# Two-convolution residual steps and an attention block on one core: the second convolution by six products in plain fp32, one image after the other, and the residual added by accumulating transfers

## What is computed

```python
for _ in range(3):
    t = relu(_conv(x, w1) + b1[None, :, None, None])
    x = x + 1/3 * (_conv(t, w2) + b2[None, :, None, None])
x = relu(x)
qkv = einsum('oc,bchw->bhwo', qkv_w, x)          # 8 heads of 8
k = _ln(k, kln_w, kln_b);  v = _ln(v, vln_w, vln_b)
kv = einsum('bhnd,bhne->bhde', k, v) / N
o = einsum('bhnd,bhde->bhne', q, kv)
u = gelu(einsum('oc,bchw->bohw', o1_w, o + x))
return gelu(einsum('oc,bchw->bohw', o2_w, u) + x)
```

## Time and profile before

| | us |
|---|---|
| median of 3 runs (lowest, highest) | 1809.97 (1804.1, 1812.8) |
| span of the profiled execution | 1808.4 |
| its own time by the clock of the runs | not listed apart; the span is 1.6 under the median and inside the runs' range |
| PE busy | 1760.9 (97% of the span) |
| DVE busy | 1268.9 (70%) |
| ACT busy | 916.9 (51%) |
| POOL busy | 1.8 |

### The profile page before, as it was taken

How to read it: one execution, slowest core, us unless ns; L and a number is a source line. 1 busy time by engine, 2 the same in 40 slices (tenths; PEclk the granted TensorE clock), 3 DMA queues, 4 the chain that set the end, 5 groups by cost and what they waited for, 6 DMA issues and landing times.

```text
span 1808.4 us, 30258 instructions
## 1 busy us (share of the span) xinstructions
PE 1760.9 (97%) x10875; PEld 1613.7 (89%) x10875; DVE 1268.9 (70%) x2481; ACT 916.9 (51%) x1533; POOL 1.8 (0%) x16
## 2 busy tenths in 40 slices
PE   7999999999999999999999999999999999999995
PEld 6998989989899898998989989898899989999884
DVE  4674668857687676876668676696666957679585
ACT  3453636446454464545545455454455545455473
POOL 0000000000000000000000000000000000000000
PEclk9999999999999999999999999999999999999997
DMA  3110002020021101111020110201102010000102
GB/s 56 27 22 0 1 1 48 13 36 3 16 33 24 24 3 25 30 19 24 3 41 14 18 25 1 47 7 24 20 1 48 13 24 13 1 1 13 30 7 47
DMA packets 135415, 36.17 MB, mean 20 GB/s; under 512 B 135116, under 2 KB 135116, under 8 KB 135244
## 3 DMA queue, kind: packets, MB, share of 16 engines
q1 hardware_dynamic: 135164, 33.82, 11.2%
q10 hardware_dynamic: 80, 0.15, 0.0%
HBM read 17.17 MB, written 16.78 MB: 19 GB/s over the span
## 4 chain that ended last, share of the span: by engine, by line
PE 87%; DVE 7%; issue 4%; ACT 1%; DVEq 0%; DMA 0%; ACTq 0%
PE bank L900 27%; PE bank L901 26%; PE bank L902 26%; PE bank L996 3%; PE bank L984 2%; PE bank L986 2%; PE bank L985 2%; DVE v_lo L770 1%; DVE combined L737 1%; DVE combined L741 1%; DVE combined L738 1%; DVE x_lo L770 1%; DVE combined L742 0%; DVE kv L793 0%; PE bank L1014 0%
## 5 line engine op out<-in xcount | busy, mean ns | idle before, releaser
L900 PE MATMUL bank<-x_hi,w_hi 128*128 128x448 f32 (+2 forms) x1440 | 517.2, 359 | 13.9 <-issue 7.4
L901 PE MATMUL bank<-x_lo,w_hi 128*128 128x448 f32 (+2 forms) x1440 | 511.4, 355 | 0.0
L902 PE MATMUL bank<-x_hi,w_lo 128*128 128x448 f32 (+2 forms) x1440 | 511.2, 355 | 0.0
L900 PEld LDWEIGHTS bank<-x_hi,w_hi 128*128 128x128 f32 x1440 | 273.2, 190 | 32.2 <-issue 12.6
L901 PEld LDWEIGHTS bank<-x_lo,w_hi 128*128 128x128 f32 x1440 | 273.4, 190 | 15.1
L902 PEld LDWEIGHTS bank<-x_hi,w_lo 128*128 128x128 f32 x1440 | 272.5, 189 | 15.3
L494 ACT ACTIVATE drain<-bank,b_col 128x448 f32<-128x448 f32 (+1 forms) x160 | 98.1, 613 | 254.7 <-PE bank L902 253.9
L500 ACT ACTIVATE drain<-bank 128x512 f32<-128x512 f32 x256 | 154.8, 615 | 107.3 <-PE bank L902 104.6
L719 DVE TENSOR_TENSOR combined<-drain 128x448 f32<-128x448 f32 (+1 forms) x160 | 95.8, 598 | 105.9 <-ACT drain L494 99.5
L770 DVE TENSOR_TENSOR v_lo<-combined,v_hi 128x896 fp32r<-128x896 f32 (+1 forms) x160 | 165.1, 1032 | 0.3
L900 PE MATMUL bank<-t_hi,w_hi 128*128 128x512 f32 x384 | 156.1, 407 | 0.0
(11 more groups left out here) (144 smaller groups left out, 3259.7 us busy)
## 6 DMA issues: line engine op xcount, KB each, us to landing
x_in<-in_x SPq DMA_DIRECT2D x64, 256.0 KB, 4.7
out<-y SPq DMA_DIRECT2D x120, 128.0 KB, 2.6
out<-drain SPq DMA_DIRECT2D x8, 128.0 KB, 2.7
x_res<-in_L_conv_w ACTq DMA_DIRECT2D x1, 144.0 KB, 2.9
x_res<-in_L_conv_w SPq DMA_DIRECT2D x1, 144.0 KB, 5.1
b_col<-in_L_conv_b SPq DMA_DIRECT2D x4, 0.2 KB, 3.0
g<-in_L_conv_o_w SPq DMA_DIRECT2D x3, 16.0 KB
g<-in_L_conv_qkv_w SPq DMA_DIRECT2D x2, 16.0 KB
```

The lines of the kernel that those rows point to most:

```text
L900: mm(ps, lhs[0], rhs[0], start=first, stop=False)
L901: mm(ps, lhs[0], rhs[1], start=False, stop=False)
L902: return mm(ps, lhs[1], rhs[0], start=False, stop=last)
```

## The change

The order of passes is now step 0 image 0, step 0 image 1, step 1 image 0 and so on: a pass is the 5 chunks of the first convolution and then the second convolution in 2 halves of 16 groups, 7 chunks a pass and 42 a pair. All six passes transform: six inputs give four outputs, so a half is 6 products x 2 stacks = 12 matmuls of 256 columns, each a single matmul in plain fp32, in 3 PSUM units of 4. No high and low parts of t exist any more. DVE makes the six planes of t in two sets (`transform_t`: 21 groups behind chunk 2 of a pass, 12 behind chunk 4; 7 instructions each), and the four outputs of each half (`combine_m`, 8 instructions) into `dx`. POOL then issues a transfer that adds `dx` to `x_res` in SBUF (512 KB each, 12 a pair), and ACT and DVE split the new `x_res` (`refresh_hi`, `refresh_lo`, 1024 elements each) 3 and 4 chunks later. ACT also copies the loaded x into `x_res` (`copy_x`). The two conv-input splits, the attention's arithmetic and the loads and stores stay; the `LATE` table has new chunk numbers.

```diff
-SIZES = ((7, 7, 7, 6, 6), (8, 8, 8, 8))
-AHEAD = (1, 2)
+CONV0_SIZES = (7, 7, 7, 6, 6)
+HALVES = 2
+UNITS = [3 if is_conv1(n) else 1 for n in range(NC)]
+PRODUCTS = (1, 2, 3, 4, 0, 5)
+SETS = ((0, 21), (21, SKEWED))
+SET_AFTER = {2: 0, 4: 1}
+REFRESH = (3, 4)
...
-        (NORMALISE, 0, (4, 5, 7, 8, 10, 10, 11, 11)), (OUTER, 0, (6, 7, 9, 10, 11, 12, 12, 13)),
+        (NORMALISE, 0, (5, 6, 7, 7, 8, 10, 10, 11)), (OUTER, 0, (6, 7, 8, 8, 10, 11, 11, 12)),
...
+            with pool.Fori(0, PAIRS) as i:
+                for number in range(NH):
+                    img, h = number // HALVES % 2, number % HALVES
+                    pool.wait_ge(dx_made, i * NH + number + 1)
+                    pool.sem_inc(add_begun, 1)
+                    nc.gpsimd.dma_start(x_res[img][:, HALF_PX * h:HALF_PX * (h + 1)], dx[h][:, :],
+                                        accum_op=ALU.add).then_inc(x_added[h], 16)
...
+            def refresh_hi(i, number):
+
+                img, step, h = number // HALVES % 2, number // HALVES // 2, number % HALVES
+                act.wait_ge(x_added[h], 16 * (i * PASSES + number // HALVES + 1))
...
+            def convolve_conv1(i, n):
+                g0, size = groups_of(n)
...
+                pe.wait_ge(v_made, i * NH + half_number(n) + 1)
+                for part in range(3):
+                    unit = UNIT[n] + part
+                    bank_free(i, unit)
+                    for k in range(2):
+                        q = PRODUCTS[2 * part + k]
+                        ps = conv_ps[unit % CONV_BANKS][:, k * PLANE:(k + 1) * PLANE]
+                        for stack in range(2):
+                            last = mm(ps, fw[:, q, 1 - stack, :], v_all[:, KEPT.index(q), g0 + stack:g0 + stack + size, :],
+                                      start=stack == 0, stop=stack == 1)
+                    last.then_inc(conv_ready, 1)
...
             def iteration(i, attends, splits, first=False):
                 for n in range(NC):
-                    take_conv(i, n)
+                    if is_conv1(n):
+                        combine_m(i, n)
+                    elif PART[n] in SET_AFTER:
+                        transform_t(i, n)
+                    for number in REFRESH_AT[n]:
+                        refresh_lo(i, number)
```

More of the change, by code:

```diff
@@ L78 @@
[L78 to L86, removed]
+CONV0_SIZES = (7, 7, 7, 6, 6)
+HALVES = 2
+HALF_GROUPS = GROUPS // HALVES
+HALF_PX = HALF_GROUPS * COLS
+TILES = COLS // 4
+PLANE = HALF_GROUPS * TILES
@@ new lines, with img_of, step_of, is_conv1 @@
+PER_CONV0 = len(CONV0_SIZES)
+PER_PASS = PER_CONV0 + HALVES
+PASSES = 2 * STEPS
+NC = PASSES * PER_PASS
+NH = PASSES * HALVES
+PASS = [n // PER_PASS for n in range(NC)]
+PART = [n % PER_PASS for n in range(NC)]
+def img_of(n):
+    return PASS[n] % 2
+def step_of(n):
+    return PASS[n] // 2
+def is_conv1(n):
+    return PART[n] >= PER_CONV0
+def half_of(n):
+    return PART[n] - PER_CONV0
+def half_number(n):
+    return PASS[n] * HALVES + half_of(n)
+def groups_of(n):
+    if is_conv1(n):
+        return half_of(n) * HALF_GROUPS, HALF_GROUPS
+    return sum(CONV0_SIZES[:PART[n]]), CONV0_SIZES[PART[n]]
@@ L89 @@
 CONV_BANKS = 3
 RING = 4
[L91 to L118, removed]
@@ L148 @@
-X_SPLIT = ({43: 0, 45: 1}, {0: 0, 2: 1})
-PROJECT, DEVIATION, INVERT, NORMALISE, OUTER, FOLD, UP, DOWN, FINISH = (
-    "project", "deviation", "invert", "normalise", "outer", "fold", "up", "down", "finish")
+PRODUCTS = (1, 2, 3, 4, 0, 5)
+KEPT = (1, 2, 3, 4, 5, 0)
+SETS = ((0, 21), (21, SKEWED))
+SET_AFTER = {2: 0, 4: 1}
+SET_ROWS = max(b - a for a, b in SETS)
+ROW = COLS // 2 + 2
+REFRESH = (3, 4)
+FIRST_REFRESH = {(half_of(n) + HALVES * PASS[n], n + REFRESH[half_of(n)]) for n in range(NC) if is_conv1(n)}
@@ L155, in steps @@
+REFRESH_AT = {n: [h for h, at in sorted(FIRST_REFRESH) if at == n] for n in range(NC + max(REFRESH))}
+X_SPLIT = ({39: 0, 40: 1}, {4: 0, 5: 1})
+PROJECT, DEVIATION, INVERT, NORMALISE, OUTER, FOLD, UP, DOWN, FINISH, REFRESH_X = (
+    "project", "deviation", "invert", "normalise", "outer", "fold", "up", "down", "finish", "refresh")
 def steps(kind, img, *numbers):
@@ L953, in convolve, with bank_free @@
                 last.then_inc(conv_ready, 1)
+            def convolve_conv1(i, n):
+                g0, size = groups_of(n)
+                if i_is(i, 0) and n == PER_CONV0:
+                    pe.wait_ge(weights_split, 2)
+                pe.wait_ge(v_made, i * NH + half_number(n) + 1)
+                for part in range(3):
+                    unit = UNIT[n] + part
[7 more added lines that the diff above has]
+                    last.then_inc(conv_ready, 1)
+            def bank_free(i, unit):
+                if not (i_is(i, 0) and unit < CONV_BANKS):
+                    pe.wait_ge(drained, i * NU + unit - CONV_BANKS + 1)
             def ring_free(a, s, uses):
```

552 lines of the change are left out of this document (273 added, 279 removed).

## The result

The changed kernel takes 1858.87 us (median of four runs, 1857.42 to 1865.01) against 1808.18 for the kernel before on the same chip: ratio 1.0281, 95% interval 1.0255 to 1.0307. The profiled execution took 1859.72 us with a span of 1857.6. One of the four runs of experiment 2 (1915.31 us at a mean granted clock of 0.834, the others at 0.967 and more) fell in the chip's slower state and is left out of its figures.

A forecast was written before the change was run, and what follows sets the result against it. It took PE's stream to bound the kernel. Pair 0 -11, six middle pairs +62, last pair +11 and tail +12 gave +74: span 1882, about 1885 us; range 1845 to 1925, chance 0.62.

The forecast's parts named there:

- What PE saves: PE's second convolutions in a pair: 80.1 us before, 68.3 after at 0.474 a matmul, saving 11.8 a pair.
- The waits: PE waiting in a middle pair for steps behind DVE's long pieces or for banks: 22.6 us.
- The clock: PE at half speed behind long waits, 1 to 1.5 us a stretch: 2.0 a pair added.
- The sum: Whole run: pair 0 -11, six middle pairs +62, last pair +11, tail +12, together +74; about 1885 us.
- the sign that PE's busy time falls by about 90: Expected in the profile: PE busy about 90 us less while its idle time rises to some 170.
- The tail: End of the run behind the last convolutions: 53.5 us before, 65.7 after, +12.
- PROJECT 4 of the last pair: In chunk 39 of the last pair, PROJECT 4 waits 4.6 us for a refresh behind set 0 and DOWN 3.
- The accumulating transfers: POOL's transfers adding dx to x_res: about 5 to 9 us each, costed at nothing.
- The cover in a middle pair: From the combination's end in chunk 40 to ACT's refresh: 10.5 us tightest; a pass without attention has 9.5.
- Rival 1: PE is saved 11.8 a pair and its waits stay as today's: 1725 us; chance 0.16.
- Rival 2: A plain fp32 record costs one column time, so PE saves 34 more a pair: about 1680 us; chance 0.07.
- Rival 3: The adds take over 10 us and hold up ACT, then PE; at 15 us about 2100; chance 0.08.

The follow-up runs named there:

- experiment 2: The changed kernel with UP and DOWN of image 1 one chunk later each: 1837.33 us, ratio 1.0162 to the kernel before.
- run 1: The changed kernel with DVE doing a chunk's INVERT and NORMALISE ahead of its combine_m or transform_t: 1768.22 us, ratio 0.9786 to the kernel before.
- run 5: The changed kernel with DVE doing INVERT, NORMALISE and FOLD's first and last step ahead of the chunk's convolution work: 1703.51 us, ratio 0.9427.
- run 9: The kernel before with INVERT, NORMALISE and FOLD's first and last step ahead of the taking of a chunk's banks: 1808.6 against 1808.86 us.
- run 10: The changed kernel with only FOLD's first and last step ahead, the normalising left where it is: 1807.14 us, ratio 0.9984 to the kernel before.

## Why the prediction was right

The forecast was 1885 and slower; measured 1859. The direction and its reason were right; that the size came out within 1.4% is in part luck, since two errors of over 4 us a pair nearly cancel. The mechanism is the one predicted, shown by runs 1, 5, 9 and 10 (take the waits away and the change is 5.7% faster, while the kernel before doesn't gain). Step by step:

- **What PE saves.** Predicted 11.8 a pair, at 0.474 us for a plain fp32 matmul. It is two records, as I took it, but 48 records go by in 10.36 us, 0.432 a matmul. That is 6.0 a pair more (144 matmuls). By the busy times it is less: PE's busy time in a pair at full clock fell from 217.9 (three of the five whole pairs of the kernel before; the other two have a stretch at half speed and 219.4) to 201.2, by 16.6, so 4.8 more than the 11.8. The 1.2 between the two ways of counting I didn't place. My own range had 0.43 a matmul as its lower end.
- **The waits.** Predicted 22.6, measured 20.9 in the pair from 704.10:

| chunk | for | predicted | measured |
|---|---|---|---|
| 7 | NORMALISE 1 | 3.2 | 2.76 |
| 21 | the same, image 1 | 3.2 | 2.63 |
| 24 | NORMALISE 4 | 3.0 | 3.01 |
| 31 | FOLD 0 | 2.4 | 2.27 |
| 33 | FOLD 3 | 5.0 | 4.67 |
| 6, 11, 14, 27 | small ones | 3.3 | 3.5 |
| 40, 41 | banks, set 1 | 2.5 | 2.0 |

  Walking the three engines' orders with durations from rows placed every wait. That of chunk 21 came out shorter since `combine_m` took 3.34, not 3.5, and INVERT 1.99, not 2.1. In chunk 7 two errors meet: DVE began `combine_m` only at 907.73, 2.3 behind the end of the half and not 0.9, with a split of `x_lo` (906.59, 1.22) in front, and PE came later too, by its own wait of 1.28 in chunk 6.
- **The clock.** Predicted 2.0 a pair, measured 6.8 in the mean, 0.6 of which the kernel before had already: the second mis-sized term. I had tied a chance of losing the clock to each wait by its length, which fails both ways: behind the wait of 3.01 it stayed full in four of six pairs, and behind that of 2.27 it fell in two. A stretch also cost more than my 1 to 1.5: the half behind the wait of 4.67 alone took 1.7 longer. The Trainium skill (TensorE: Matmul & The Clock Gate, the section on HAM oscillation), by which I had estimated 5.5, was nearer than I was; but not all waits of that size have their stretch at a time, as its rule read for each gap would have it.
- **The sum.** Per middle pair, in the means: 220.8, less 0.6 of clock, less 16.6 of stream, plus 20.8 of waits for 2.3, plus 6.8 of clock: 228.8 where I had 231.2. The errors in stream and clock, 4.8 and 4.2, nearly cancel; that in the waits is 1.7. So it is with the sign that PE's busy time falls by about 90: it fell by 90.1, but as a larger saving less a larger loss of clock. Six middle pairs cost 1373.0 - 6 x 220.8 = +48 (predicted +62). The tail is 65.2 against 53.6, +12, just as predicted. Pair 0 and the last pair together come out at -11 (predicted 0), what remains of +49. The faster matmul accounts for 10 to 12 of the difference; and PROJECT 4 of the last pair waited 2.13 for VectorE, not 4.6. The rest I didn't split.
- **The accumulating transfers.** Costed at nothing: right, but for one wait of 1.8 us of ScalarE in the tail. Their duration, 4.7 us in the median, is below my 5 to 9. The Trainium skill's fit (DMA: Bandwidth & Descriptors, anatomy of a GpSimd DMA) had given an estimate of 3.2; the measurement decides. The cover in a middle pair is 9.5 and 10.2 where I had 9.5 and 10.5; in pair 0, without attention, it is 8.3.
- **The rivals.** Rival 1 didn't come about by itself: the waits it left out are there. Its 1725 is near what the change gives once they are taken away (run 5: 1704, with a matmul cheaper than it assumed). Rival 2 is excluded by the records. Rival 3 is excluded here; its price was too low: three adds in a row, some 16 us (issued at 728.41, 733.65 and 740.12), cost 465 us and not 215. PE's mean clock was 0.879 there; how much of the 465 is clock and how much the banks hid less than the half I gave them, I didn't separate.

## What to carry over

When a change replaces short pieces on a helper engine by long ones, PE's saving is known at once, and the loss has to be walked: for each step for which the main engine waits, add up what stands in front of it in the helper's queue. If the sum is over what PE has to do meanwhile, do the short, awaited step first; here that was worth 155 us and cost two lines. An order that was good before says nothing about the order after.

Judge an edit of waits together with the clock, and by all pairs and not by one: pairs of one run with the same waits differed by up to 5.8 us. Here taking or filling one of five long waits gave back its idle time at best and 0.5 of the clock's 6.8 us a pair at most; taking two gave back 1.4; with three gone more than half of it went, and with all five gone all of it.

## What I hadn't expected of the hardware

- The clock's price did not fall by a fixed part for each wait taken away: 6.8 us a pair with five waits of over 2 us, 6.8 and 6.3 with four, 5.4 with three, 3.0 with two, nothing with none. Which of the waits the loss follows changes from pair to pair. What picks the place is left open; no run here tells it.
- The length of a pause alone doesn't decide it. In the kernel before, the clock was at 0.50 from 1084 to 1086, behind a pause of PE of 1.93 at 1083.05; and in run 5 it stayed at 1.00 through pauses of 5.12 and 3.32 in the first 10 us.
- A plain fp32 matmul of 256 columns costs 0.432 us in a stream (two records of 0.216), 3.6 times the 0.1185 of an fp32r one of the same size, and not 4.
- A transfer of 512 KB within SBUF that adds to its target took 4.7 us from issue to landing in the median (4.5 to 7.4; medians of 4.6 to 4.9 in the other runs), as long as 256 KB from HBM in the kernel before. Those loads got slower beside them: 6.1 us in the median instead of 4.7. PE's list of waits has none for a load.
